# Four gather passes of a graph network: one of every 40 row tiles fetched by SyncE instead of GpSimd

## The reference

```python
# layer 0, twice (GCN): msg = h[s] * norm; out = segment_sum(msg, d)
# layer 1:
neigh_sum = jax.ops.segment_sum(features[src], dst, num_segments=N)
# layer 2 (weighted edges):
msg = x_lin[row] * norm[:, None]
out = jax.ops.segment_sum(msg, col, num_segments=N)
# layer 3: hihj = concatenate([x[src], x[dst]]); attention over edges, segment_sum of the messages
```

## Time and profile before

| | us |
|---|---|
| median of 3 runs | 11311.23 |
| lowest and highest | 11309.79, 11313.01 |
| profiled execution, its own time | 11313.72 |
| its span, first to last instruction | 11311.9 |
| GpSimd busy | 8218.0 (73%) |
| TensorE busy | 4272.0 (38%) |
| gathers of passes 0 to 2 | 4689, 946 ns each |
| gathers of pass 3 | 1563, 947 ns each |
| gathers of pass 4 | 1563, 960 ns each |

### The profile page before, as it was taken

How to read it: one execution, slowest core, us unless ns; L and a number is a source line. 1 busy time by engine, 2 the same in 40 slices (tenths; PEclk the granted TensorE clock), 3 DMA queues, 4 the chain that set the end, 5 groups by cost and what they waited for, 6 DMA issues and landing times. The chain is left out here.

```text
span 11311.9 us, 80457 instructions
## 1 busy us (share of the span) xinstructions
PE 4272.0 (38%) x19462; PEld 2951.7 (26%) x19462; DVE 3426.1 (30%) x7384; ACT 3212.1 (28%) x7261; POOL 8218.0 (73%) x8365
## 2 busy tenths in 40 slices
PE   1222222342222223223333433333354433344687
PEld 0111111121111112111111333333354333333576
DVE  4000001110001112000000422222235677777898
ACT  3333333343333334333333300000021111111465
POOL 5777777757777775777777677777766777777676
PEclk5555555565555556555555655566665555555799
DMA  4222222222222223222222222221214555555453
GB/s 104 79 79 79 79 79 79 75 87 79 79 79 79 79 79 101 79 79 79 79 79 79 62 53 53 53 53 53 53 47 136 159 159 165 164 166 168 148 170 134
DMA packets 676194, 1069.57 MB, mean 95 GB/s; under 512 B 150850, under 2 KB 518729, under 8 KB 648857
## 3 DMA queue, kind: packets, MB, share of 16 engines
q0 software_dynamic: 329072, 676.05, 22.9%
q10 hardware_dynamic: 247712, 225.10, 6.1%
q1 hardware_dynamic: 98985, 163.50, 4.4%
HBM read 904.63 MB, written 161.05 MB: 94 GB/s over the span
## 5 line engine op out<-in xcount | busy, mean ns | idle before, releaser
L448 POOL DMA_INDIRECT big<-table_parts,tile_cols x4689 | 4436.4, 946 | 1591.0 <-issue 1427.4
L601 PE MATMUL psum<-big 128*128 x4992 | 1723.0, 505 | 4113.0 <-SPq L457 3659.4
L601 PEld LDWEIGHTS psum<-big 128*128 128x128 bf16 x4992 | 672.0, 141 | 5094.2 <-issue 2874.0
L448 POOL DMA_INDIRECT big<-ptable,tile_cols x1563 | 1500.8, 960 | 498.4 <-issue 476.0
L448 POOL DMA_INDIRECT big<-table,tile_cols x1563 | 1480.1, 947 | 478.5 <-issue 476.0
L556 ACT ACTIVATE big<-big,ones 128x2048 bf16<-128x2048 bf16 x312 | 624.4, 2001 | 3689.3 <-PE psum L601 2458.7
L549 ACT ACTIVATE big<-iota_col,dl_tab 128x128 bf16<-128x128 f32 x4992 | 1490.6, 387 | 33.4 <-PEq L725 12.9
L1612 PE MATMUL psum<-acc,big 128*128 x3328 | 784.5, 418 | 1211.2 <-DVE big L1588 1199.1
L578 DVE TENSOR_REDUCE acc<-psum 128x128 f32<-128x384 f32 (+1 forms) x196 | 109.7, 560 | 3635.1 <-PE psum L604 1820.3
L673 PE MATMUL psum<-big 128*128 x3328 | 752.8, 419 | 1194.1 <-SPq L457 740.7
L1612 PEld LDWEIGHTS psum<-acc,big 128*128 128x128 f32 x3328 | 700.8, 315 | 1294.7 <-issue 1294.3
(11 more groups left out here) (299 smaller groups left out, 4284.9 us busy)
## 6 DMA issues: line engine op xcount, KB each, us to landing
big<-dl_rows ACTq DMA_DIRECT2D x104, 1024.0 KB
zrows<-big ACTq DMA_DIRECT2D x104, 1024.0 KB, 5.5
big<-zrows SPq DMA_DIRECT2D x104, 1024.0 KB, 4.9
big<-table_parts,tile_cols POOLq DMA_INDIRECT x4689
table_parts<-big SPq DMA_DIRECT2D x42, 672.0 KB, 3.5
big<-table,tile_cols POOLq DMA_INDIRECT x1563
big<-ptable,tile_cols POOLq DMA_INDIRECT x1563
ptable<-big SPq DMA_DIRECT2D x14, 455.0 KB, 4.1
```

What stands on the lines that cost most here:

```text
L448: pool.indirect_dma_start(out=slots[:, t % (groups * GT), 0:width], out_offset=None, in_=tab, in_offset=bass.IndirectOffsetOnAxis(ap=idx_t ...
L601: last = nc.tensor.matmul(held, m, rows_t, start=False, stop=False, skip_group_check=True)
```

## The change

In passes 0 to 3 GpSimd leaves out the last tile of the groups 8, 13, 18, ... 188, which are 37 groups. SyncE fetches these tiles itself, each by 128 transfers of one row into one partition. The address of each transfer comes out of a register; the register values are byte offsets (row number times row size), kept in a new SBUF tile `side_numbers` that the set-up fills by two more loads and two more VectorE operations. SyncE issues the 128 transfers in five portions of 25 or 26, a portion at the end of each of the five iterations that precede the announcement of the tile's group. The slot it writes is the one that the group eight places earlier gave back in the first of these iterations. All 128 transfers of a tile count on one semaphore, `s_side`, which SyncE waits for (2048) and clears before it announces the group. `LEAD` goes from 4 to 3. `s_steps` is folded into `s_bias`. The bytes that move stay the same: 128 rows of 768 bytes (512 in pass 3) a tile.

```diff
-LEAD = 4
+LEAD = 3
+SIDE_FIRST, SIDE_EVERY = 8, 5
...
+    SIDE = list(range(SIDE_FIRST, TGROUPS - RGROUPS + LEAD + 1, SIDE_EVERY))
+    SIDE_SPAN = SIDE_EVERY * GT * P
+    SIDE_BASE = (SIDE_FIRST + 1) * GT * P - SIDE_SPAN
...
+        side_tab = sb("side_numbers", [64 + len(SIDE), P], i32)
+        side_of = [side_tab[64 * k:64 * k + len(SIDE), :] for k in range(2)]
...
+        def has_side(no, g):
+
+            return no < PASSES - 1 and g in SIDE
...
-                for k in range(tiles_of(g)):
+                for k in range(tiles_of(g) - has_side(no, g)):
...
-        def relay_rows(sp, no, groups, lead, s_done, done0):
+        def relay_rows(sp, no, groups, lead, s_done, done0, fetch_side=None):
 
             def landed(g):
                 sp.wait_ge(gathered[g % RGROUPS], landed_count(no, g))
+                if has_side(no, g):
+                    sp.wait_ge(s_side, 16 * P)
+                    sp.sem_clear(s_side)
                 sp.sem_inc(s_landed[no], 1)
...
                     sp.wait_ge(s_done, releases[g % 4] + done0)
                     sp.sem_inc(s_free, 1)
+                    if fetch_side:
+                        fetch_side(sp, g)
+
+        def side_rows(no, tab, slots, width, kind, row_bytes):
+
+            flat, size = tab.rearrange("n f -> (n f)").unsqueeze(0), row_bytes // width
+
+            def fetch(sp, g):
+                k, j = g // SIDE_EVERY, g % SIDE_EVERY
+                if k >= len(SIDE):
+                    return
+                t = SIDE[k] * GT + GT - 1
+                e0, e1 = j * P // SIDE_EVERY, (j + 1) * P // SIDE_EVERY
+                words = [nc.alloc_registers(f"side{no}_{g}_{e}", engines=[SP]) for e in range(e0, e1)]
+                nc.regs_load(words, side_of[kind][k:k + 1, e0:e1])
+                for e in range(e0, e1):
+                    at = nc.snap(words[e - e0], engines=[SP], donate=True, min_val=0, max_val=(N - 1) * row_bytes,
+                                 guaranteed_mod_val=0, out_of_modulus=row_bytes)
+                    sp.dma_start(slots[e:e + 1, t % RSLOTS, 0:width], flat[:, bass.ds(at // size, width)]).then_inc(s_side, 16)
+
+            return fetch
...
+                side_src = src[SIDE_BASE:SIDE_BASE + len(SIDE) * SIDE_SPAN].rearrange("(k s) -> k s", s=SIDE_SPAN)[:, SIDE_SPAN - P:]
+                for to in side_of:
+                    sp.dma_start(to, side_src).then_inc(s_last, 16)
...
-                dve.wait_ge(s_last, 32)
-                step = Steps(dve, s_dve, 0, 3)
+                dve.wait_ge(s_last, 64)
+                nc.vector.tensor_scalar(side_of[0], side_of[0], 2 * NPARTS * F, None, ALU.mult)
+                step = Steps(dve, s_dve, 0, 4)
+                step(nc.vector.tensor_scalar(side_of[1], side_of[1], 4 * F, None, ALU.mult))
```

More of the change, by code:

```diff
@@ L58, in gnn_kernel @@
     ALU, ACT, AX = mybir.AluOpType, mybir.ActivationFunctionType, mybir.AxisListType
-    DVE, PE = mybir.EngineType.DVE, mybir.EngineType.PE
+    DVE, PE, SP = mybir.EngineType.DVE, mybir.EngineType.PE, mybir.EngineType.SP
     N, E = x.shape[0], src.shape[0]
@@ L77, in gnn_kernel @@
     NTAB = NI + BODY
+    SIDE = list(range(SIDE_FIRST, TGROUPS - RGROUPS + LEAD + 1, SIDE_EVERY))
+    SIDE_SPAN = SIDE_EVERY * GT * P
+    SIDE_BASE = (SIDE_FIRST + 1) * GT * P - SIDE_SPAN
+    assert SIDE_FIRST == RGROUPS and RGROUPS - SIDE_EVERY == LEAD and SIDE_BASE + len(SIDE) * SIDE_SPAN <= E
     CHUNKS = NW // CW
@@ L273, in gnn_kernel @@
         s_dve, s_cnt, s_wt, s_wrows, s_bias = (sem(n) for n in (
-            "setup_dve", "degree_rooted", "weights_transposed", "weights_copied", "biases"))
+            "setup_dve", "degree_rooted", "weights_transposed", "weights_copied", "biases_and_steps"))
         s_cmp, s_counted, s_starts, s_degrees, s_idx, s_conv, s_low, s_in, s_ptr, s_item = (sem(n) for n in (
@@ L280, in gnn_kernel @@
         s_dlrow, s_tr, s_kept, s_dlkept = (sem(n) for n in ("dl_row", "transposed", "weights_kept", "dl_kept"))
-        s_steps = sem("step_table")
         s_dlout = [sem(f"dl_out{h}") for h in range(2)]
@@ L430, in gnn_kernel @@
         s_free = sem("rows_free")
+        s_side = sem("side_rows")
         def tiles_of(g):
             return min(GT, NT - g * GT)
+        def has_side(no, g):
+            return no < PASSES - 1 and g in SIDE
         def landed_count(no, g):
-            whole = sum(tiles_of(k) for k in range(g % RGROUPS, TGROUPS, RGROUPS))
-            return 16 * (no * whole + sum(tiles_of(k) for k in range(g % RGROUPS, g + 1, RGROUPS)))
+            return 16 * sum(tiles_of(k) - has_side(n, k) for n in range(no + 1)
+                            for k in range(g % RGROUPS, g + 1 if n == no else TGROUPS, RGROUPS))
         def gather_tiles(pool, no, tab, slots, groups, width):
@@ L541, in _ @@
                 def _(sp):
-                    relay_rows(sp, no, RGROUPS, LEAD, s_prod, items0)
+                    relay_rows(sp, no, RGROUPS, LEAD, s_prod, items0, side_rows(no, table16, ring16, NPARTS * F, 0, 2 * NPARTS * F))
                 @block.scalar
@@ L626, in _ @@
                 def _(sp):
-                    relay_rows(sp, no, RGROUPS, LEAD, s_prod, items0)
+                    relay_rows(sp, no, RGROUPS, LEAD, s_prod, items0, side_rows(no, table, ring32, F, 1, 4 * F))
                 @block.vector
@@ L824, in _ @@
                 sp.dma_start(SUM_AT[:, 0:NI], sum_t[:, 0:P]).then_inc(s_win, 16)
-                sp.dma_start(STEP_AT[:, 0:NI], step_t[:, 0:P]).then_inc(s_steps, 16)
+                sp.dma_start(STEP_AT[:, 0:NI], step_t[:, 0:P]).then_inc(s_bias, 16)
                 sp.wait_ge(s_added, PSLOTS)
@@ L834, in _ @@
                     parts.store(sp, c, c % 4)
-                sp.wait_ge(s_steps, 16)
+                sp.wait_ge(s_bias, 64)
                 sp.dma_start(STEPS[:, 0:M_STEPS].bitcast(i16), STEP_AT[:, M_GROUP:M_GROUP * M_STEPS + 1:M_GROUP]).then_inc(s_win, 16)
-                sp.wait_ge(s_bias, 48)
                 sp.wait_ge(s_win, 13 * 16)
@@ L909, in _ @@
                         ln.relu(act, t - 1, (t - 1) % 2)
-                act.wait_ge(s_dve, 15)
+                act.wait_ge(s_dve, 16)
                 nc.scalar.activation(deg_r, deg, ACT.Sqrt).then_inc(s_cnt, 1)
@@ L946, in _ @@
                 dve.wait_ge(s_starts, 1)
-                step = Steps(dve, s_dve, 3, 10)
+                step = Steps(dve, s_dve, 4, 10)
                 step(nc.vector.tensor_tensor(bound[:, 0:NW], bank[5][:, 0:NW], wplus1[:, 0:NW], ALU.add))
@@ L1030, in _ @@
                         keep_dl(t - 2)
-                step = Steps(dve, s_dve, 3 + 10, 3)
+                step = Steps(dve, s_dve, 4 + 10, 3)
                 dve.wait_ge(s_degrees, 1)
@@ L1058, in _ @@
                 last.then_inc(s_counted, 1)
-                pe.wait_ge(s_dve, 3)
+                pe.wait_ge(s_dve, 4)
                 nc.tensor.matmul(bank[5][:, 0:NW], first, tile_cnt[:, 1:NW + 1], start=True, stop=True).then_inc(s_starts, 1)
```

## The result

The changed kernel takes 13513.6 us (median of 4 runs, 13484.4 to 13545.4) against 11311.1 before: a ratio of 1.195, 95% interval 1.191 to 1.198. It is 2202 us slower, where 184 us less was forecast, and lies outside the range.

What follows compares the result with a forecast made beforehand. GpSimd's gathers, one every 1.25 us, were taken as the bound. Removing 148 gave -185 us, set-up +1, sum -184: 11127 us; SyncE's X of 49.5 stayed under the 49.75 limit. Range 11110 to 11900 us.

Steps and rivals of the forecast that it cites:

- X: SyncE's queue in passes 0 to 3: its time for five groups, 49.5 us, or 14.0 + 128c with step c.
- The removed gathers: GpSimd in passes 0 to 3: 148 gathers fewer at 1.25 us each, 185 us less.
- What bounds the kernel, and the budget: GpSimd's gapless gathers, 48.8 us per five groups; ring slack lets X reach 49.75, beyond it 148 us per microsecond.
- The register loads: SyncE's five loads of 25 or 26 words per fetched tile: 9.8 us together, 27.4 us at the other end.
- Rival B: SyncE's register loads are slow, 214 ns a word: X = 67.1, about 13690 us; chance 0.10.
- The step of a transfer: SyncE's one-row issues: 0.277 us each, bounds 0.26 and 0.40, 35.5 us for 128; a register address seems free.
- The last row and the rest: SyncE before announcing the tile's group: 2.0 us for the last row; 2.2 us for release values, semaphores and gaps.
- LEAD 3: SyncE's announcement of a group to TensorE comes one iteration later relative to a release: costs nothing.
- late announcements: TensorE hears of groups later while SyncE is in a portion of some 9 us; its 1156.2 us of waiting covers that.
- the transfers on the DMA engines: Same bytes, engines 0.29 busy in passes 0 to 2; rival D, rows queueing behind each other in transfer, had chance 0.03.
- Set-up: Two more loads and two VectorE operations before the passes: +1 us, bounds 0 and 3.
- A: SyncE becomes the bound and GpSimd waits for `rows_free`, from c = 0.289; mostly below +590 us; chance 0.29.

Runs made afterwards that it cites:

- e4_no_fetch: The changed kernel with GpSimd leaving out the 37 tiles of each pass and SyncE fetching nothing in their place: 11128.0 us, ratio 0.984 to the kernel before.
- e2_shifted: The changed kernel with portions of 24 and 28 rows and the byte-offset table begun 8 bytes off a multiple of 16: 14531.3 us.
- e1_aligned: The changed kernel with portions of 24, 28, 24, 28 and 24 rows, so each register load starts at a multiple of 16 bytes: 11769.5 us, ratio 1.040.
- e11_fixed_third: The changed kernel with constant transfer addresses, no register loads or moves, on a chip where the kernel before takes 11307.1 us: 11131.5 us, ratio 0.985.
- e3_every6: The changed kernel with aligned portions of 20 and 24 rows, one fetched tile in six groups and LEAD 2: 11159.2 us, ratio 0.986.
- e8_lead3_again: The kernel before with LEAD 3 in place of 4 and nothing else, on a slower chip: 12850.2 us, ratio 0.9998.

## Why the prediction was wrong

The step that failed is X, SyncE's time for five groups: 49.5 us were added up, 65.8 measured. Two of its terms were too small, the register loads and the step of a transfer; the path, the budget that X was held against and the price of going beyond it were right.

- *The removed gathers*, -185 us: right (e4_no_fetch, -186.6).
- *What bounds the kernel, and the budget*: right. GpSimd's 48.8 us for five groups, the ring's slack that puts the limit at 49.75 us, and 148 us for each microsecond beyond gave +2190, +459 and, with 72.8 us a cycle for e2_shifted, +3227 against +2202, +455 and +3217 measured.
- *The register loads*: the term that failed most. 9.8 us were taken, 20.2 measured; the 10.4 us are 1540 of the result. I had both rates in the earlier trace rows, but sorted them by the size of a value, and asked only whether the count was a multiple of four. For the two aligned loads that gave the right price, 1.84 and 2.04 us against 1.85 and 2.03; the other three were 5.3 to 5.5. All tables with the fast rate are also read from starts that are multiples of 32 bytes. The size of a value plays its own part: SyncE's loads of four two-byte values start by turns at a multiple of 16 bytes and 8 off it, and take 0.855 us either way. Rival B took the slow rate for all five, 27.4 us, and was too high because two of the starts are aligned. The rule of the Trainium skill that the prediction quoted, about 200 ns a register even in bulk ("Runtime: NRT & Kernel Launch", section "Instruction fetch mechanics"), holds in e2_shifted, (5.91 - 5.10)/4 = 0.20 us a word, and fails in e1_aligned, (1.83 - 1.61)/4 = 0.055.
- *The step of a transfer*: 0.277 us taken, 0.327 measured; 50 ns, 6.4 us a cycle, 950 us of the result. Two errors. I went below SyncE's own row of 0.29, and e11_fixed_third then showed 0.294. And I called a register address free because the store itself took as long; the trace of the kernel before has 12 moves of 29 ns as instructions of their own on the same line, ahead of the stores with a register's address, and I read only the line of the DMA. The step from start to start would have shown it.
- *The last row and the rest*: 2.0 us taken, 1.05 measured; 2.2 taken for release values and semaphores, 2.7 left over as the remainder. The load of release values took 1.05 us in place of 0.855, also in the aligned versions. Small.
- *LEAD 3, late announcements, the transfers on the DMA engines*: nothing to be seen, as forecast (e4_no_fetch, e3_every6, e11_fixed_third). *Set-up*: +1 forecast, too small to be seen.
- *Two slips*: A's first price, -185 + 148 x 1.6, is +52 and not +59. The two loads of the earlier trace rows, issued 0.34 us apart, landed 2.6 and 3.0 us after their issues, so some 0.7 us apart and not within 0.4. Nothing hung on either.
- *The chances*: A had 0.29 and B 0.10, and the case of both together, which came, was not in the list. The step of 0.327 us with aligned loads is e1_aligned, +455, inside the range. B's 13690 us is close to the 13513.6 measured by luck: its loads were 7.2 us a cycle too high and its step 6.4 too low. So it is with the 2100 us by the Trainium skill's rule: loads 5.4 us too high, the step again 6.4 too low.

So the mechanism was that of rival A, SyncE as the bound, with part of B in the loads. The prediction called the forecast a knife edge, 0.01 us of a step deciding the sign. By the measured terms it wasn't one: the loads alone, with the step of 0.277 us, make X 59.9 and the result +1317 us; the step alone makes 55.9 and +725.

## What to carry to other kernels

An engine that waits 95% of the time has room, but the room is spent by its queue's instructions one after the other: count the moves and the loads that feed a DMA, and take the step from start to start, not the duration of one line. Load four-byte values into registers from SBUF at starts that are multiples of 16 bytes; it was worth 1744 us here. Where a relay also carries work of its own, compute its cycle against that of the engine it relays for, and space the work so that it fits: a cycle of some 55 us (estimated from the terms above) against 58.8 left SyncE waiting for gathers 10% of the time. Each alone wasn't enough: +19.5% became +4.0% by alignment in five groups, +7.3% was left with six groups and no alignment, and both together gave -1.4%.

## What the runs showed of the hardware that was not expected

- A load of 24 four-byte words from SBUF into SyncE's registers takes 1.61 us from a start at a multiple of 16 bytes and 5.10 us from one 8 bytes off. In the changed kernel starts 4 and 12 bytes off are as slow (5.52 us for 26 words, 5.31 for 25).
- A one-row transfer holds SyncE's queue 0.252 us with a constant address and 0.225 with a register's, but the move ahead of it makes the step 0.318 against 0.294 us.
- About every 60 transfers with their moves, some 120 instructions, one step is about 0.33 us longer: 284 steps, 93 us, which make 5 of the 9 ns between the median of 0.318 and the mean of 0.327. The queue that brings instructions carried 551 packets of 8 KB in place of 249:

```profile
q14 instruction: 551, 4.51, 0.1%
```

  302 packets for 38,633 further instructions, one for 128. In e11_fixed_third, which has no moves, such a step comes about every 114 transfers, 141 in all, and the queue carried 397 packets, 148 more for 18,947 further instructions: again one for 128. That these steps are the change from one packet to the next fits all four counts, but isn't shown.
- Two of the chips run the kernel before in 12850 to 12865 us, 13.7% longer, with a like granted clock (0.595 in the profile of e8_lead3_again against 0.597). The slow stretches are not SyncE's alone. In that profile ScalarE's neighbouring instructions of L549 start at 804.12, 804.83, 805.56, 806.26, 809.05 and 810.47 us, and 1019 instructions of TensorE's queue, 103 of ScalarE's and 20 of SyncE's are followed by the next after 0.7, 1.4, 2.1 or 2.8 us, to within 6 ns; in the kernel before on the chip of 11311 us these are 1, 1 and 2. So on these chips the passes wait for TensorE's products even with no row fetched by SyncE. Why the instructions come late isn't known. A relay filled to 80% (e11_fixed_third) fits on one kind of chip and not on the other.
